# Cross-attention kernel: four matrix products cut into 64 by 64 pieces that alternate between the column tiles of TensorE

## What is computed

```
x1n = ln(x) * g + b;  c_n = ln(context);  f_n = ln(fside)
out_s = softmax((x1n Wq)(c_n Wk)^T / sqrt(128)) (c_n Wv) Wo + bo      for s = audio (context), video (fside)
res   = out_a + out_v + x
x1    = ln(res) @ fc_W + fc_b + res
out   = x1 + softmax((x1 Wq1)(context Wk1)^T / sqrt(128)) (context Wv1) Wo1 + bo1   (per sequence after the batches are regrouped by 64)
```

## The kernel before

| stage (line) | product, per group | read by |
|---|---|---|
| zT (1387), cfT (1397), prob0T (1426), resT (1455), x1T (1470), prob1T (1494) | transposes of 128 by 128, four a group (prob1T two) | ACT |
| t0 (1406) | `m0` (128 by 128) against 512 columns, one product | ACT |
| s0 (1416), mix0 (1437) | 16 products, 64 rows, 64 weight columns, 64 moving columns | DVE; ACT |
| mix1 (1503) | 8 products of the same form | ACT |
| s1 (1486) | 8 products, 65 rows, 64 weight columns, 64 moving columns | DVE |
| out0 (1447), dense (1462) | 4 products each, 128 by 128 against 128 columns | DVE |
| t1 (1476) | 65 weight columns against 512 columns, one product | ACT |
| out1 (1511) | 2 products, 64 rows, 128 weight columns, 256 moving columns | DVE |

## Time and profile before

### The profile page before, as it was taken

How to read it: one execution, slowest core, us unless ns; L and a number is a source line. 1 busy time by engine, 2 the same in 40 slices (tenths; PEclk the granted TensorE clock), 3 DMA queues, 4 the chain that set the end, 5 groups by cost and what they waited for, 6 DMA issues and landing times.

```text
span 190.3 us, 6538 instructions
## 1 busy us (share of the span) xinstructions
PE 167.8 (88%) x2310; PEld 122.1 (64%) x2310; DVE 148.7 (78%) x562; ACT 139.2 (73%) x390; POOL 120.3 (63%) x247
## 2 busy tenths in 40 slices
PE   0278987999989999999999999999999999999752
PEld 0256566766658586867786778685878687676321
DVE  6998299999999999899768578557685959955531
ACT  3054686788988969969899976996987767565640
POOL 2298639888989898998788989995616142022000
PEclk9999999999999999999999999999999999999965
DMA  5999999001000200021200220020202201010131
GB/s 177 326 250 253 303 388 360 17 0 32 1 3 0 81 5 7 3 83 58 87 29 2 88 83 3 14 72 13 77 0 88 82 6 59 0 55 5 55 113 57
DMA packets 8962, 15.87 MB, mean 83 GB/s; under 512 B 1313, under 2 KB 1570, under 8 KB 8930
## 3 DMA queue, kind: packets, MB, share of 16 engines
q1 hardware_dynamic: 8482, 15.18, 24.8%
q10 hardware_dynamic: 448, 0.27, 0.6%
HBM read 11.25 MB, written 4.19 MB: 81 GB/s over the span
## 4 chain that ended last, share of the span: by engine, by line
PE 65%; DVE 22%; issue 4%; ACT 3%; DMA 3%; ACTq 1%; DVEq 0%
PE ps_d L1462 7%; PE ps_z L1406 6%; PE ps_p L1447 5%; PE ps_d L1476 5%; PE ps_g L1511 5%; PE ps_r L1486 4%; PE ps_s L1416 4%; PE ps_d L1470 4%; DVE stats L933 4%; PE ps_g L1437 4%; DVE stats L926 3%; PE ps_z L1387 3%; PE ps_p L1426 3%; DMA w_sb<-in_w 3%; PE ps_r L1455 3%
## 5 line engine op out<-in xcount | busy, mean ns | idle before, releaser
L393 POOL TENSOR_TENSOR rstd<-st_var,minus_half 128x12 f32<-128x12 f32 x14 | 31.9, 2280 | 0.2 <-DVE stats L933 0.2
L619 ACT ACTIVATE z_sb<-x_sb,shift,rstd 128x128 f32<-128x128 f32 x64 | 26.4, 491 | 0.2 <-POOL shift L402 0.2
L1051 DVE SCALAR_TENSOR_TENSOR x_sb<-ps_d,rstd,res_sb 128x128 f32<-128x128 f32 x64 | 17.9, 341 | 7.5 <-PE ps_d L1462 6.6
L682 ACT ACTIVATE ps_r<-ps_r,minus_max 128x64 f32<-128x64 f32 x64 | 18.5, 290 | 2.2 <-DVE minus_max L1059 2.2
L1462 PE MATMUL ps_d<-w_fc,resT_sb 128*128 128x128 f32 x128 | 18.5, 288 | 0.0
L451 POOL TENSOR_TENSOR rstd<-v_var,minus_half 128x4 f32<-128x4 f32 x7 | 7.1, 1011 | 18.0 <-DVE v_var L1043 18.0
L1406 PE MATMUL ps_z<-zT_sb,m 128*128 128x512 f32 x32 | 17.8, 640 | 0.0
L1447 PE MATMUL ps_p<-w,mix_sb 128*128 128x128 f32 x128 | 17.3, 278 | 0.3 <-ACT mix_sb L655 0.3
L933 DVE BATCH_NORM_STATS2 stats<-cf_sb 128x6 f32<-128x64 f32 x128 | 17.5, 210 | 0.0
L1447 PEld LDWEIGHTS ps_p<-w,mix_sb 128*128 128x128 f32 x128 | 15.8, 191 | 2.5 <-issue 1.5
L1476 PE MATMUL ps_d<-x1T_sb,m 128*65 128x512 f32 x32 | 16.7, 602 | 0.0
(11 more groups left out here) (154 smaller groups left out, 433.0 us busy)
## 6 DMA issues: line engine op xcount, KB each, us to landing
x_sb<-in_x SPq DMA_DIRECT2D x16, 256.0 KB, 5.8
cf_sb<-in_cf SPq DMA_DIRECT2D x16, 256.0 KB, 6.2
out<-out_sb SPq DMA_DIRECT2D x16, 256.0 KB, 2.0
ct_sb<-in_ct SPq DMA_DIRECT2D x16, 128.0 KB, 3.2
w_sb<-in_w SPq DMA_DIRECT2D x1, 384.0 KB
w_score_sb<-in_w_score ACTq DMA_DIRECT2D x1, 128.0 KB, 5.0
w_sb<-in_w ACTq DMA_DIRECT2D x1, 128.0 KB, 5.9
wt_sb<-in_wt SPq DMA_DIRECT2D x1, 96.0 KB
```

The source lines that it names most:

```text
L393: pool.tensor_tensor(rstd0[:, slot, :], st_var[:, g % SLOTS, :], minus_half[:, :], ALU.pow).then_inc(rstd0_done, 1)
L619: last = nc.scalar.activation(z_sb[:, g % Z_SLOTS, p, :], x_sb[:, g, p, :], ACT.Identity, bias=shift0[:, slot, p:p + 1], scale=rstd0[:, sl ...
L682: last = nc.scalar.activation(ps_r[:, p * S:(p + 1) * S], ps_r[:, p * S:(p + 1) * S], ACT.Exp, bias=minus_max1[:, slot, p:p + 1], accum_ou ...
L1051: last = v.scalar_tensor_tensor(x1_sb[:, g % SLOTS, p, :], ps_d[:, p * D:(p + 1) * D], rstd1[:, g % SLOTS, p:p + 1], res_sb[:, g % RES_SLO ...
```

## The change

t0, out0, dense and out1 are each cut into 16 products of 64 weight columns by 64 moving columns. In t0, out0 and dense, which have 128 rows, successive products go to the two column halves in turn, as in s1. In out1, which has 64 rows, they go round the four 64 by 64 tiles, as in s0, mix0 and mix1. The results lie where they lay before; the waits, the semaphores, the order of the stages and all other engines are as they were.

```diff
@@ t0
-                mm(ps_z[:, :], m0[:, :], zT_sb[:, g % SLOTS, :], start=True, stop=True).then_inc(t0_made, 1)
+                for at in range(0, PAIRS * P, S):
+                    for half in HALF:
+                        last = mm(ps_z[half, at:at + S], m0[:, half], zT_sb[:, g % SLOTS, at:at + S],
+                                  start=True, stop=True)
+                last.then_inc(t0_made, 1)
@@ out0
-                        last = mm(ps_p[:, p * P:(p + 1) * P], mix0_sb[:, g % SLOTS, u, v, :, :], w0[:, :],
-                                  start=True, stop=True)
+                        for n in HALF:
+                            for b in range(2):
+                                last = mm(by_pair(ps_p[HALF[b], :])[:, p, n], mix0_sb[:, g % SLOTS, u, v, b, :],
+                                          w0[:, n], start=True, stop=True)
@@ dense
-                    last = mm(ps_d[:, p * P:(p + 1) * P], resT_sb[:, g % SLOTS, p * P:(p + 1) * P], w_fc[:, :],
-                              start=True, stop=True)
+                    for n in HALF:
+                        for b in range(2):
+                            at = (2 * p + b) * S
+                            last = mm(by_pair(ps_d[HALF[b], :])[:, p, n], resT_sb[:, g % SLOTS, at:at + S], w_fc[:, n],
+                                      start=True, stop=True)
@@ out1
-                for u in range(DUOS):
-                    last = mm(ps_g[:, u, 0:2 * P], w1[HALF[u], :], mix1_sb[HALF[u], g % SLOTS, :, :, :],
-                              start=True, stop=True)
+                for v in range(2):
+                    for b in range(2):
+                        at = (2 * v + b) * S
+                        for u, m in TILES:
+                            last = mm(ps_g[HALF[m], u, at:at + S], w1[HALF[u], HALF[m]],
+                                      mix1_sb[HALF[u], g % SLOTS, v, b, :], start=True, stop=True)
```

## The result

The changed kernel takes 194.24 us in the median of 8 runs (192.74 to 194.47), the kernel before, on the same chip, 191.53. The ratio is 1.0118, with a 95% interval of 1.0083 to 1.0152: slower by 1.6 to 2.9 us. A second set of runs gave 1.0129 (1.0088 to 1.0169). The forecast was 194.9 in a range of 192.4 to 198.0, slower. The direction came out as forecast, and so did the sum of the middle of the program, though in part by luck; the growth of TensorE's work and what leaks out of the first third were taken too large.

The account below looks back on a forecast made before the run. TensorE was taken as the bound from 67.5 to 160.9 us, DVE before, single stages in turn after. 1.0 + 2.2 + 0.3 = 3.5 us on a median of 191.41 gave 194.9 us, range 192.4 to 198.0.

Parts of the forecast that it names:

- TensorE is full from 67.5 us on: From 67.5 to 160.9 us TensorE is busy 92.8 of 93.4 us, so each added piece of its time lengthens the run.
- The pace with 128 rows: Inside the new t0, out0 and dense, MATMULs start 29 ns apart as in s1; bounds 15 and 111 ns.
- Rival 2: t0, out0 and dense at the four tiles' pace, 0.50 us each; some 180 us results; chance 0.05.
- The stages themselves grow by 0.25 us per group: t0 grows 0.11, out0 and dense 0.08 each, out1 shrinks 0.02: 4.0 us over 16 groups.
- the border between different tile forms: Stages of different tile forms meet in 40 places instead of 15, each paying an exit of 0.12 us.
- the exit of 0.12: Leaving a tile form on TensorE costs 0.12 us; exits go from 73 to 95, +2.6 us.
- The theory of borders: Cost is a sum over stages of their pace and over borders between array forms, the borders being most of it.
- The middle stretch: From 67.5 to 160.9 us: stages 2.4, exits +1.4, entries -0.5, full behind tiled -1.1; 2.2 us, all on the path.
- The first stretch: Up to 67.5 us TensorE's work grows 2.9 us against 4.3 idle; 1.0 taken as reaching the path, bounds 0 and 2.9.
- The end: From 160.9 us the work sums to nothing, but the last dense's result comes later; 0.3 us taken.
- Rival 3: Small products far slower, from exposed weight loads (one in four is 21 us, 216) or an unfed queue; chance 0.06.
- The rule of about 25 ns: Start-to-start never below about 25 ns; the new out1 would take 0.78 us instead of 0.50, the sum 4.5 us higher.

Follow-up runs that it names:

- the experiments with single parts: Kernel before with one hunk of the change alone: t0 1.0152, out0 1.0084, dense 1.0018, out1 0.9981.
- the second profile: The changed kernel run once more, unaltered, for another profile: 1.0129 against the kernel before, profiled time 194.59 us.
- t0 undone: The changed kernel with t0 back in its full form, out0, dense and out1 still new: 1.0141 against the kernel before, +2.7 us.
- the case shown: s0 of group 6 one stage later, in the kernel before with only out1 new and eight swaps of neighbouring stages: 1.0161, +3.1 us.

## Why the prediction was right or wrong

- **TensorE is full from 67.5 us on, so its work is what counts: right, but only from 90 us on.** 92.9 of 93.4 us are busy after as before, but up to 90 us the work that came on top still went into short waits.
- **The pace with 128 rows is s1's, 29 ns: right.** It was the unknown, bounded by 15 and 111. The stages came out at 0.93 to 1.08. Rival 2 is out; alternation is what gives the pace.
- **The stages themselves grow by 0.25 us per group, borders give the rest: the size of the sum was too high**, 4.9 against 4.2 counted from the lengths in the traces. The term that was mis-sized is the border between different tile forms. I paid the exit of 0.12 (the new stages have 0.10, those on four tiles 0.11) and missed that a stage behind its own form also takes 0.05 less, in 32 places after against 6 before. These 26 places alone are 1.3 us. About 0.7 of it was made up by the stages themselves, which grow by 0.30 per group and not 0.25 (0.98 without the exit, where I took 0.96 to 0.97). The theory of borders itself held, and the experiments with single parts show it: dense +0.3, out0 +1.6 for the same product.
- **The middle stretch gives 2.2: right in sum, not in its parts, and so in part luck.** The work grew by 1.7 by the count. In this profile 0.7 of the 2.2 are the pauses at fetched blocks, which stand nowhere in my sum; the second profile has 1.9 with 0.6 of pauses. Without them 1.5 and 1.3 are left.
- **The first stretch leaks 1.0 of 2.9: wrong.** 0.3 to 0.4 of 2.7 leaked. The range 0 to 2.9 held it; the argument that little idle time left must make DVE late did not. The added work filled short waits of TensorE, of 0.1 to 0.3 us each, at single stages (behind t1 of group 0 0.34 less was idle, behind t1 of group 2 0.29 less).
- **The end gives 0.3: wrong by little,** it gave about nothing (-0.1).
- **The whole:** 1.0 + 2.2 + 0.3 = 3.5 was forecast, 0.4 + 2.2 - 0.1 = 2.4 from the first zT on was found, and the timed runs have 2.3.
- **Rival 3, a queue that isn't fed: right in kind, wrong in size.** Its 21 us were those of exposed loads, and the feeding had no price of its own. It is there, as pauses that add 0.2 to 0.9 us to a stage. The load in average instructions (22 ns each) did not show it, since it strikes at block borders.
- **The rule of about 25 ns from start to start** (the Trainium skill, page "TensorE: Matmul & The Clock Gate", section "Wait — 56ns, not 53.3ns?") would have made out1 0.78 us; it takes 0.52 in front of its own form. This trace disagrees with it.

Left open: why t0 undone is timed at +2.7 us when its profile has +1.7. More pauses in the timed runs would do it, but the timed runs have no trace. Open is also why some packets land late.

## What to carry to other kernels

Count the forms of the array along TensorE's queue before cutting a product into tiles. A 128 by 128 product in four pieces on two column tiles runs at the rate of the whole one at best (116 against 111 ns), and here a stage of another form among full ones costs about 0.24 us in borders (0.15 in itself, 0.09 in the stage before it). So such a cut can pay only beside stages of the same form, as out1 beside s0 and mix0, and there the gain (0.4 us) wasn't told from nothing. In a hand-written order move only a stage whose reader is late anyway; in the case shown a swap saved 0.11 us of borders and kept a reader waiting for 0.9.

## What the runs showed of the hardware that was not expected

Successive MATMULs of 64 moving columns on one column tile of 64 start 58 ns apart and on two in turn 29, with a weight load for each; on two in turn it is so with 65 rows and with 128. A stage on two column tiles behind its own form starts its second pair after 58 to 60 ns, behind another form after 107. In five of the six profiles of kernels with three or four parts changed, TensorE's queue paused for 0.2 to 0.8 us at a fixed place in a block of 256 instructions, each time where the last packet of the fetch queue had landed at most 1.3 us before.
